# Causal attention with 8-wide heads: q and k as two f32r parts on 32-row groups, stacks filled from SBUF, mask added by VectorE

## What is computed

```python
q = (x @ q_w + q_b).reshape(Bx, Tx, NH, HD).transpose(0, 2, 1, 3)
kv = (x @ kv_w + kv_b).reshape(Bx, Tx, 2, NH, HD).transpose(2, 0, 3, 1, 4)
att = jnp.einsum('bhqd,bhkd->bhqk', q, k) * (1.0 / np.sqrt(HD))
att = att + build_alibi_bias(NH, Tx)[None]
att = jnp.where(causal[None, None], att, -jnp.inf)
att = jax.nn.softmax(att, axis=-1)
y = jnp.einsum('bhqk,bhkd->bhqd', att, v)
x = _layernorm(x + y.transpose(0, 2, 1, 3).reshape(Bx, Tx, Cx) @ o_w + o_b, axis=-1)
```

## Time and profile before

| what | us |
|---|---|
| median of 3 runs | 1357.54 (1357.23 to 1358.01) |
| the profiled execution | 1353.68 |
| its span, first to last instruction | 1351.6 |
| TensorE, matmul busy | 1178.0 |
| VectorE busy | 853.8 |
| ScalarE busy | 774.2 |
| GpSimd busy | 605.8 |

### The profile page before, as it was taken

How to read it: one execution, slowest core, us unless ns; L and a number is a source line. 1 busy time by engine, 2 the same in 40 slices (tenths; PEclk the granted TensorE clock), 3 DMA queues, 4 the chain that set the end, 5 groups by cost and what they waited for, 6 DMA issues and landing times. The chain is left out here.

```text
span 1351.6 us, 30224 instructions
## 1 busy us (share of the span) xinstructions
PE 1178.0 (87%) x9378; PEld 846.6 (63%) x9444; DVE 853.8 (63%) x2155; ACT 774.2 (57%) x1659; POOL 605.8 (45%) x1064
## 2 busy tenths in 40 slices
PE   2789999999999999999998728969999899998974
PEld 1445455545554555455554328959999799997864
DVE  3887878777877787878775254453333255563775
ACT  1166666666666666666666604556666566665442
POOL 0044434443444344444444406777600145551687
PEclk9799999999999999999999958989999999998998
DMA  6644343434343434244331043213322233332222
GB/s 156 145 120 117 77 105 89 112 80 103 94 110 74 108 97 107 75 103 103 92 93 28 9 113 112 82 64 103 107 58 59 60 86 106 102 106 72 73 85 73
DMA packets 144008, 123.63 MB, mean 91 GB/s; under 512 B 21625, under 2 KB 130361, under 8 KB 143674
## 3 DMA queue, kind: packets, MB, share of 16 engines
q1 hardware_dynamic: 128350, 99.14, 28.9%
q0 software_dynamic: 8192, 16.79, 4.1%
q10 hardware_dynamic: 7356, 6.29, 1.9%
HBM read 73.14 MB, written 44.04 MB: 87 GB/s over the span
## 5 line engine op out<-in xcount | busy, mean ns | idle before, releaser
L528 ACT ACTIVATE probs<-scores 128x512 f32<-128x512 f32 x640 | 363.5, 594 | 181.2 <-PE scores L444 175.7
L566 POOL TENSOR_SCALAR_AFFINE_SELECT probs<-probs 128x256 f32<-128x256 f32 (+1 forms) x640 | 237.6, 378 | 371.6 <-ACT probs L528 367.0
L426 PE MATMUL maxed<-kstack,qstack 96*128 96x512 bf16 (+3 forms) x1024 | 272.1, 307 | 24.9 <-DMA kstack<-k_parts 20.2
L992 DVE TENSOR_TENSOR e_hid<-e_gate,e_up_ps 128x352 f32<-128x352 f32 x208 | 108.1, 520 | 216.3 <-ACT e_gate L1250 188.3
L444 PE MATMUL scores<-qstack,kstack 128*128 128x384 bf16 (+3 forms) x960 | 213.6, 295 | 16.9 <-ACT probs L528 13.6
L700 DVE TENSOR_REDUCE maxA<-maxed 128x4 f32<-128x512 f32 x256 | 175.2, 685 | 71.2 <-PE maxed L428 70.7
L428 PE MATMUL maxed<-causal,identb 128*128 128x128 bf16 x1024 | 195.6, 223 | 0.0
L426 PEld LDWEIGHTS maxed<-kstack,qstack 96*128 96x128 bf16 x1024 | 101.0, 99 | 149.3 <-issue 58.9
L460 PE MATMUL pv<-probs,vaug 128*32 128x512 f32 (+3 forms) x2048 | 190.7, 445 | 0.1
L1173 PE MATMUL e_gate_ps<-e_w_in,e_xT 128*128 (+1 forms) x624 | 161.0, 367 | 23.5 <-DVE e_xT L997 22.5
L700 DVE TENSOR_REDUCE maxB<-maxed 128x4 f32<-128x512 f32 x256 | 174.0, 680 | 4.4 <-PE maxed L428 4.4
(11 more groups left out here) (159 smaller groups left out, 1715.1 us busy)
## 6 DMA issues: line engine op xcount, KB each, us to landing
qstack<-q_parts SPq DMA_DIRECT2D x64, 288.0 KB
kstack<-k_parts SPq DMA_DIRECT2D x192, 96.0 KB
x_sorted<-zeros SPq DMA_DIRECT2D x32, 288.0 KB, 4.3
e_xs<-x_sorted SPq DMA_DIRECT2D x144, 64.0 KB
y_sorted<-e_raw_down SPq DMA_DIRECT2D x144, 64.0 KB, 1.9
q_parts<-parts SPq DMA_DIRECT2D x16, 384.0 KB
k_parts<-parts SPq DMA_DIRECT2D x48, 128.0 KB
xin<-in_x SPq DMA_DIRECT2D x16, 256.0 KB, 5.3
```

The lines of the kernel that those rows point to most:

```text
L426: pe.matmul(bank[:, col:col + (i + 1) * P], q[0:MAX_ROW, h, i * P:(i + 1) * P], ks[0:MAX_ROW, h, 0:(i + 1) * P], start=True, stop=False)
L528: act.activation(probs[g % 2][:, u * T:(u + 1) * T], scores[(UNITS * g + u) % SB][:], ACT.Exp).then_inc(S["exp_done"], 1)
L566: pool.affine_select(out=view, in_=view, compare_op=ALU.is_ge, fill=0.0, base=0, pattern=pattern, channel_multiplier=-1).then_inc(S["maske ...
L992: dve.tensor_tensor(hid[k][:, 0:F], gate[k][:], up_ps[k][:, 0:F], ALU.mult).then_inc(S["hid_done"], 1)
```

## The change

- q and k are cut into two f32r parts, high and rest. The high part is written by ScalarE from `misc` with the bias (the scale is in `wq` now); VectorE writes the rest as `misc` + bias - high. `whole`, `rest` and GpSimd's part are gone.
- A head's contraction has 24 rows for three products (high-high, high-rest, rest-high), 2 for the position bias, 2 for the maximum and 3 that cut blocks of 32 keys inside a diagonal tile. It fits in 32 partitions, so four heads lie one under another on the four row groups, in four slots: `qstack` and `kstack` are [128, 4, 512] f32r, three buffers each. Heads 2j and 2j + 1 share a row group (`place_of`). The host lays out the weights' columns to match (`laid_out`).
- SP fills a stack with 24 transfers from `parts` in SBUF, all at the start of the step; nothing goes through DRAM.
- The causal matmul is gone. `take_max` adds the mask and takes the maximum in one `tensor_tensor_reduce` for each block, 64 a sequence, which writes to `rowmax` at once; the combining instructions are gone.
- In `unit` the diagonal tile has a matmul of its own with the cut rows, and the rest of the width one without.

```diff
+ROW_TILES, SLOTS, ROWS = 4, 4, 32
+STACKS = 3
+PARTS, TERMS = 2, 3
+Q_PARTS, K_PARTS = (0, 0, 1), (0, 1, 0)
...
+def place_of(h):
+
+    return h // 2 % ROW_TILES, h // 8 * 2 + h % 2
...
-JOBS = (("xt", "q", "k", "qr", "kr"), ("y0", "y1", "y2", "y3", "v"), ("yn", "o", "ln", "x1t"), ("m", "mr", "lg"))
+JOBS = (("xt", "q", "k"), ("y0", "y1", "y2", "y3", "v"), ("yn", "o", "ln", "x1t"), ("m", "lg"))
...
+                    for w, (stack, order) in enumerate(((qstack[buffer], Q_PARTS), (kstack[buffer], K_PARTS))):
+                        sp.wait_ge(S["qk_high"], st.at(2, 2, w + 1))
+                        sp.wait_ge(S["qk_low"], st.at(2, 2, w + 1))
+                        for tile in range(ROW_TILES):
+                            for n, part in enumerate(order):
+                                row = ROWS * tile + HD * n
+                                sp.dma_start(stack[row:row + HD, :, :].bitcast(F32),
+                                             parts[tile * HD * SLOTS:(tile + 1) * HD * SLOTS, w, part, :].bitcast(F32)) \
+                                    .then_inc(done, 16)
...
-                        pe.matmul(bank[:, col:col + (i + 1) * P], q[0:MAX_ROW, h, i * P:(i + 1) * P],
-                                  ks[0:MAX_ROW, h, 0:(i + 1) * P], start=True, stop=False)
-                        last = pe.matmul(bank[:, col + i * P:col + (i + 1) * P], identb[:], causal[:],
-                                         start=False, stop=True)
+                        rows, slot = rows_of(h, MAX_ROW)
+                        last = pe.matmul(bank[:, col:col + (i + 1) * P], q[rows, slot, i * P:(i + 1) * P],
+                                         ks[rows, slot, 0:(i + 1) * P], start=True, stop=True)
...
-                                last = pe.matmul(scores[n % SB][:, col:col + width],
-                                                 kstack[st.par(0)][:, h, kt * P:(kt + 1) * P],
-                                                 qstack[st.par(0)][:, h, kt * P:T], start=True, stop=True)
+                                rows, slot = rows_of(g * QUAD + hh, CUT_ROW + CUTS)
+                                last = pe.matmul(scores[n % SB][:, col:col + P], ks[rows, slot, keys],
+                                                 q[rows, slot, keys], start=True, stop=True)
+                                if width > P:
+                                    rows, slot = rows_of(g * QUAD + hh, CUT_ROW)
+                                    last = pe.matmul(scores[n % SB][:, col + P:col + width], ks[rows, slot, keys],
+                                                     q[rows, slot, (kt + 1) * P:T], start=True, stop=True)
...
+                        act.activation(parts[:, w, 0, :], misc[:], ACT.Identity,
+                                       bias=(qb_scaled if w == 0 else kb)[:, 0:1]).then_inc(S["qk_high"], 1)
...
+                        dve.wait_ge(S["qk_high"], st.at(2, 2, w + 1))
+                        if not st.first(2):
+                            dve.wait_ge(stack_loaded[st.stack(1)], st.loaded(1))
+                        dve.scalar_tensor_tensor(parts[:, w, 1, :], misc[:], (qb_scaled if w == 0 else kb)[:, 0:1],
+                                                 parts[:, w, 0, :].bitcast(F32), ALU.add, ALU.subtract).then_inc(S["qk_low"], 1)
...
+                    for h, i, col in blocks:
+                        (tile, slot), width = place_of(h), (i + 1) * P
+                        ins = dve.tensor_tensor_reduce(maxed[n % MB][:, col:col + width], maxed[n % MB][:, col:col + width],
+                                                       causal[:, T - width:T], 1.0, NEG, ALU.add, ALU.max,
+                                                       rowmax[st.par(off)][:, tile, slot, i:i + 1])
```

More of the change, by code:

```diff
@@ new lines, in rows_of, with by_place @@
+def rows_of(h, count):
+    tile, slot = place_of(h)
+    return slice(ROWS * tile, ROWS * tile + count), slot
+def by_place(a):
+    a = a.reshape(a.shape[:-1] + (2, ROW_TILES, 2, HD))
+    n = a.ndim - 4
+    return np.ascontiguousarray(a.transpose(*range(n), n + 1, n + 3, n, n + 2)).reshape(a.shape[:n] + (C,))
+def stack_constants():
+    q = np.zeros((ROW_TILES, ROWS - CONST_ROW, SLOTS, T), np.float32)
+    k = np.zeros((ROW_TILES, ROWS - CONST_ROW, SLOTS, T), np.float32)
+    pos = np.arange(T, dtype=np.float32)
+    for h in range(NH):
+        tile, slot = place_of(h)
+        q[tile, 0, slot], k[tile, 0, slot] = (h + 1) / NH, pos
+        q[tile, 1, slot], k[tile, 1, slot] = -pos, (h + 1) / NH
+    k[:, MAX_ROW - CONST_ROW:CUT_ROW - CONST_ROW] = 1
+    block = np.arange(T) % P // CUT
+    for r in range(CUTS):
+        q[:, CUT_ROW - CONST_ROW + r] = block == r
+        k[:, CUT_ROW - CONST_ROW + r] = np.where(block > r, NEG, 0)
+    return q, k
@@ L67, in causal_constant, with max_blocks @@
 def causal_constant():
-    mask = np.triu(np.full((P, P), NEG, np.float32), 1)
+    mask = np.zeros((P, T), np.float32)
+    mask[:, T - P:] = np.triu(np.full((P, P), NEG, np.float32), 1)
     return bf16_bits(mask)
+def max_blocks(n):
+    pair, k = divmod(n, 5)
+    if k == 4:
+        return [(2 * pair, 1, 0), (2 * pair + 1, 1, 2 * P)]
+    if k % 2 == 0:
+        return [(2 * pair + k // 2, 3, 0)]
+    return [(2 * pair + k // 2, 2, 0), (2 * pair + k // 2, 0, 3 * P)]
 def max_stage(n):
@@ L208, in attention @@
         probs = [sb(f"probs{n}", [P, UNITS * T]) for n in range(2)]
[L209 to L218, removed]
+        parts = sb("parts", [P, 2, PARTS, T], F32R)
+        rowmax = [sb(f"rowmax{n}", [P, ROW_TILES, SLOTS, QT]) for n in range(2)]
+        mparts = sb("mparts", [NH * QT, PARTS, P], F32R)
         rsum = sb("rsum", [P, NH])
@@ new lines, in _, with set_stack_rows @@
+                load("const_loaded", kb[:], io["kv_b"][0:C].rearrange("(p u) -> p u", u=1))
+                def set_stack_rows(n):
+                    for stack, rows in ((qstack[n], probs[0]), (kstack[n], probs[1])):
+                        for tile in range(ROW_TILES):
+                            at = slice(ROWS * tile + CONST_ROW, ROWS * (tile + 1))
+                            sp.dma_start(stack[at, :, :].bitcast(F32), rows[at, 0:SLOTS * T].rearrange("r (s t) -> r s t", t=T)) \
+                                .then_inc(S[f"stack_rows_loaded{n}"], 16)
@@ L435, in unit @@
                     if n == 0:
-                        pe.wait_ge(S["max_rows"], st.at(0, 48, 48))
+                        pe.wait_ge(S["max_rows"], st.at(0, 32, 32))
                     if n >= SB or not st.first(0):
@@ L527, in body @@
                                     act.wait_ge(S["pv_ready"], st.at(0, 4, g - 1))
+                                if u == 0 and st.first(0) and g < 2:
+                                    for n in range(STACKS):
+                                        act.wait_ge(S[f"stack_rows_loaded{n}"], STACK_ROWS_IN)
                                 act.activation(probs[g % 2][:, u * T:(u + 1) * T],
@@ L537, in body @@
                                 job(st, item)
-                act.dma_start(identb[:].bitcast(U16), io["identb"]).then_inc(S["masks_loaded"], 16)
+                for stack, rows in ((probs[0], io["qstack_rows"]), (probs[1], io["kstack_rows"])):
+                    for tile in range(ROW_TILES):
+                        row = ROWS * tile + CONST_ROW
+                        act.dma_start(stack[row:row + ROWS - CONST_ROW, 0:SLOTS * T],
+                                      rows[tile].rearrange("r s t -> r (s t)")).then_inc(S["stack_rows_in"], 16)
                 act.dma_start(causal[:].bitcast(U16), io["causal"]).then_inc(S["masks_loaded"], 16)
```

250 lines of the change are left out of this document (79 added, 171 removed), and 4 rows, old and new, of the table READERS.

## The result

The changed kernel takes 1599.06 us (1592.88 to 1600.44, 4 runs) where the kernel before took 1357.38 in the same comparison: ratio 1.177, 95% interval 1.174 to 1.181. It is slower, as forecast, but far above the forecast of 1396 and above the range's end of 1500.

A forecast was written before the change was run, and what follows sets the result against it. TensorE led with VectorE close behind; after the change VectorE was to be the fuller engine. 1353.7 us plus 34 (14.75 periods at +2.3) plus 5 for the prologue gave 1392.7, as median of runs 1396; range 1312 to 1500.

The forecast's parts named there:

- at a granted clock of 1.00: Attention half: TensorE's clock in a period of the kernel before, 2.4 GHz, at which all matmuls were priced.
- The sum without it: Attention period: VectorE busy 41.3 us, other waits 5.1, later q and k reads 1.2; 47.6 us, +2.3 a period.
- The term for overlap, -1.6: TensorE, maxima and scores: matmuls on different row groups run side by side, worth 0 to -3.2 us a period, half taken.
- Rival A: Attention half: faster, row groups and loads overlap, TensorE loses perhaps 7 us, period 43.4, time 1333 us; chance 0.29.
- Read-out, 0.10 us: VectorE: a second instruction reads out the maximum in each of 64 pairs, +6.4 us a period (4.8 to 15.4).
- Changes of shape, 0.05 each: TensorE around 13 jobs on `misc`: 26 changes of the array's shape a period, 0 to +2.6 us, +1.3 taken.
- Narrow f32r matmuls: TensorE: splitting off diagonal tiles raises a head's scores from 0.54 to 0.82 us, +4.5 over 16 heads.
- Prologue, +5: Before the first exponential: VectorE is the bound, 50 banks add 10 us, less 2 x 2.55 for q and k work.
- nothing there is on the path: SP's transfers: 30 issues a sequence against 27 are covered by the step and a third buffer, costing no time.
- B: TensorE: f32r takes four passes or loads are not hidden, +11.1 us a period, 1526 us; chance with C 0.19.
- C: VectorE: each read-out waits for its main instruction's end, 0.24 us, period 56.6, 1540 us; chance with B 0.19.
- D: Attention half: no change, read-out at 0.075 us and no overlap of row groups, +0.7 us a period; chance 0.06.

The follow-up runs named there:

- the version without overlap: The changed kernel with every matmul of maxima and scores contracting all 128 rows of its slot instead of 26 to 31: 1397.6 us.
- the last experiment: The changed kernel with the first of the four PV steps of each quad done three times over: 1583.4 us, a single run.
- the mask on TensorE: The changed kernel with 64 bf16 causal matmuls a sequence back on TensorE and one VectorE reduction for each bank: 2298.5 us.
- The filler ahead of each bank: The changed kernel with one more bf16 matmul of 128 rows and 512 columns ahead of each of 40 banks of maxima: 1774.4 us.

## Why the prediction was wrong

- **The clock** is the step that failed. The prediction read "at a granted clock of 1.00" off and kept it through every sum; none of its rivals had the clock in it, though the diff says 26 to 31 rows in each of the 176 matmuls of maxima and scores of a sequence. TensorE was busy 92% of a period before and 92 to 94% after, and the clock was at 1.2 GHz for 40 to 72% of it. By the Trainium skill (TensorE: Matmul & The Clock Gate, Part 1) the clock goes by how busy TensorE has been; with the busy share of the profile as the measure, these rows don't bear that out. From first to last exponential were 702.5 / 45.3 = 15.5 periods. At 44.1 to 46.0 us they would take 684 to 713; they took 929, so by this estimate the lower clock costs 216 to 245 us, about the whole loss of 226.7 there.
- **The sum without it** was 47.6 us a period. The estimate for 2.4 GHz is 44 to 46, against 45.3 before: at a full clock the change would be worth little in the attention half either way, and the sum was 1.6 to 3.5 too high. The term for overlap, -1.6, was mis-sized: in the stretch at 2.4 GHz TensorE is busy 26.3 us, and in the version without overlap, which also lacks some 26 changes of shape a period, 30.0. That is -5.6 a period by the same scaling (47.3 / 31.12). Rival A is not what happened: it let TensorE lose 7 us against the kernel before, and in that stretch TensorE is as busy as before (26.34 and 26.39). That its sum is 43.4, the number of the straight line, is chance. Nor was VectorE the fuller engine, on which the forecast rested: it is busy 25.6 us of that stretch.
- **Read-out, 0.10 us** (range 0.075 to 0.24). Measured: 1.73 a head where the four main instructions were put at 1.60. If that 1.60 holds, 0.03 is left for each read-out, under the lower bound. The bound came from small instructions that follow one another; this one hides behind its neighbour. VectorE is busy 37.7 us, not 41.3.
- **Changes of shape, 0.05 each** (0 to 0.1). Measured 0.27 a pair at 2.4 GHz, a small matmul and its load included: 26 make up to 3.5 us, not 1.3.
- **Narrow f32r matmuls.** +4.5 for the scores was about right: TensorE of the version on 128 rows is busy 46.0, where -3.8 + 0.8 + 4.5 on 41.9 give 43.4. The other 2.6 come, as I read it, with loads: 0.19 us for 128 f32r columns against 0.10 for bf16 (the mean in the two traces), which was not in the sum at widths over 128.
- **Prologue, +5.** It is +12.5, and nearly the same on 128 rows (first exponential at 81.0 and 81.4), so not the rows. The first maximum starts at 39.1 us where it started at 29.3:

```profile
13.08 1.09 PE L374 MATMUL misc<-ident,xin 128*128 128x128 f32 x4 [13.08 <-DMA xin<-in_x]
...
19.13 8.84 SPq L325 DMA_DIRECT2D qstack<-parts  x12
...
28.07 8.43 SPq L325 DMA_DIRECT2D kstack<-parts  x12
...
39.12 1.11 PE L437 MATMUL maxed<-kstack,qstack 26*128 26x512 f32 x2 [18.36 <-DMA kstack<-parts]
```

  x lands 6 us later (13.1 against 6.9) and 24 issues at 0.7 us stand ahead of the first maximum. The prediction said "nothing there is on the path"; that holds for the repeated part and not for the first sequence. This is read from the trace; no run moved the issues.
- **Rivals B, C and D.** B and C fall: 128-column score matmuls of f32r start 0.11 us apart or less at the full clock, and the read-out doesn't wait. That C's time, 1540, and B's, 1526, come nearest of all is chance. D's premise, that row groups don't overlap, is refuted by the equal starts.

Left open: no run has row tiles of 32 rows at 2.4 GHz for a whole period, so 44 to 46 stays an estimate, and the stretch that it is scaled from follows one at 1.2 GHz. Nor is it shown why full-row work raised the clock in the last experiment and not with the mask on TensorE; the second puts it in pieces of 128 columns with two changes of shape around each. Row groups by turns inside a unit or bank, which would use more rows at once, weren't tried; two groups would then write into one bank.

## What to carry to other kernels

Before a matmul's contraction is cut to a fraction of the array, put TensorE's clock into the sum as a rival of its own, with the period priced for it (here 51.7 us at a mean clock of 0.80 and 61.1 at 0.64). A busy share of 93% said nothing about it here, while the clock line of the page and an untouched instruction that has grown longer show it at once. And take a change apart: of this one, VectorE's mask alone is worth 0.8%.

## What was not expected of the hardware

- In these runs the clock goes with the rows that instructions name, not with the data on them. Mean clock of a period: 1.00 with 128 rows, also with 96 of them zero, 0.75 to 0.89 with 64 and 0.64 to 0.80 with 26 to 31 (f32r); 0.96 with all, 0.63 to 0.82 with 64 and 0.50 to 0.63 with 32 (bf16).
- Work that nobody needs can be free: 64 more matmuls a sequence, and 1583 us (a single run) in place of 1599. The filler ahead of each bank was not: 1774 us.
- Going between 32-row tiles and the whole array costs up to 0.27 us there and back at 2.4 GHz, a matmul of 16 columns and its load included, and about 0.4 at 1.2 GHz.
- The read-out of a maximum, 0.14 us by itself, costs VectorE about 0.03 us in a row of such pairs.
